# All sixteen sequences' gates of the delta rule in one batch, one write of the running decay sums, sum and cap as two operations in place

## The reference

```python
beta = jax.nn.sigmoid(bb)                          # bb, aa: [b, t, 8] projections of the normalised x
g = -jnp.exp(A_log) * jax.nn.softplus(aa + dt_bias)
alpha = jnp.exp(g)
def step(S, inp):
    q_t, k_t, v_t, beta_t, alpha_t = inp
    S = S * alpha_t[..., None, None]
    kv = jnp.einsum('bhk,bhkv->bhv', k_t, S)
    S = S + jnp.einsum('bhk,bhv->bhkv', k_t, (v_t - kv) * beta_t[..., None])
    return (S, jnp.einsum('bhk,bhkv->bhv', q_t, S))
```

## Time and profile before

| | us |
|---|---|
| three runs | 1888.81, 1888.66, 1886.35; median 1888.66 |
| the profiled execution's own time | 1888.68 |
| its span in the trace | 1887.0 (1.7 lie around it) |
| busy in the span | PE 1806.5, weight loads 1302.7, DVE 1174.6, ACT 709.8, POOL 669.4 |

### The profile page before, as it was taken

One profiled execution on the slowest core, in us unless ns is written; L12 is line 12 of the kernel. 1 busy time (PEld: TensorE's weight loads), 2 busy tenths in 40 slices (PEclk: granted clock), 3 DMA queues, 4 the chain that ended last, 5 costly groups with the idle time before them and its releaser, 6 DMA issues.

```text
span 1887.0 us, 39461 instructions
## 1 busy us (share of the span) xinstructions
PE 1806.5 (96%) x14800; PEld 1302.7 (69%) x14800; DVE 1174.6 (62%) x3215; ACT 709.8 (38%) x1887; POOL 669.4 (35%) x758
## 2 busy tenths in 40 slices
PE   6679999999889999999999999999999999999999
PEld 3357777776666666665445666666659979889698
DVE  5588888887656677677766667666665234243332
ACT  4124444444345555553001455655632222122221
POOL 3344443443216666674000376676624000000000
PEclk9879999999999999999999999999999999999999
DMA  6312212121022001010000000010040000000000
GB/s 195 53 33 49 39 34 43 37 42 26 13 79 71 25 27 36 26 35 11 1 1 1 10 29 20 20 29 20 11 179 1 3 7 1 10 1 1 10 1 10
DMA packets 98717, 58.61 MB, mean 31 GB/s; under 512 B 77801, under 2 KB 90465, under 8 KB 97761
## 3 DMA queue, kind: packets, MB, share of 16 engines
q1 hardware_dynamic: 98368, 56.03, 11.1%
q10 hardware_dynamic: 160, 0.06, 0.0%
HBM read 50.55 MB, written 5.51 MB: 30 GB/s over the span
## 4 chain that ended last, share of the span: by engine, by line
PE 81%; issue 5%; POOL 5%; DVE 4%; ACT 3%; DMA 1%; SPq 1%; DVEq 0%; POOLq 0%; ACTq 0%
PE ps L2582 18%; PE ps L1566 6%; PE ps L608 6%; PE ps L2454 5%; PE ps L1588 5%; PE ps L2114 5%; PE ps L1604 4%; PE ps L1643 4%; PE ps L1622 4%; PE ps L2660 3%; PE ps L728 2%; POOL w L580 2%; PE ps L1709 2%; PE ps L1575 2%; PE ps L1654 1%
## 5 line engine op out<-in xcount | busy, mean ns | idle before, releaser
L2027 POOL TENSOR_TENSOR h_w<-h_w 125x336 int32<-125x336 int32 x384 | 335.9, 904 | 210.4 <-ACT h_w L1808 210.4
L1912 DVE CUSTOM_DVE_ANT_0 h_w<-ps,h_w 112x375 f32<-112x375 f32 x512 | 263.3, 544 | 0.6 <-issue 0.3
L956 DVE SCALAR_TENSOR_TENSOR big_b<-ps,taps,big_b 128x444 f32<-128x444 f32 (+2 forms) x288 | 194.0, 674 | 74.9 <-ACT big_b L830 47.9
L1808 ACT ACTIVATE h_w<-ps 125x336 f32<-125x336 f32 x512 | 197.7, 468 | 21.7 <-PE ps L1588 21.7
L275 POOL TENSOR_TENSOR rstd<-var_eps,minus_half 112x4 f32<-112x4 f32 x12 | 12.2, 1015 | 406.5 <-DVE var_eps L262 406.5
L1588 PEld LDWEIGHTS ps<-h_w 32*125 32x125 f32 x3072 | 96.0, 183 | 62.1 <-issue 61.3
L1588 PE MATMUL ps<-h_w 32*125 32x112 f32 x3072 | 118.0, 282 | 7.8 <-DVE h_w L1912 5.5
L1921 DVE TENSOR_TENSOR h_w<-h_w,ps 128x112 f32<-128x112 f32 x128 | 34.7, 271 | 141.6 <-PE ps L1575 141.6
L1566 PE MATMUL ps<-h_w 32*112 32x375 f32 x1024 | 121.1, 519 | 0.8 <-DVE h_w L1912 0.8
L608 PE MATMUL ps<-h_w,w 128*128 128x448 f32 x256 | 110.3, 554 | 4.6 <-ACT h_w L852 4.6
L608 PE MATMUL ps<-h_w,kq_w 128*128 128x448 f32 x256 | 113.7, 569 | 0.0
(11 more groups left out here) (360 smaller groups left out, 3728.9 us busy)
## 6 DMA issues: line engine op xcount, KB each, us to landing
h_w<-in_h SPq DMA_DIRECT2D x2, 4096.0 KB, 17.0
kq_w<-in_ctxT SPq DMA_DIRECT2D x16, 375.0 KB, 3.4
h_w<-in_ctxT SPq DMA_DIRECT2D x16, 375.0 KB, 3.3
big_a<-decays SPq DMA_DIRECT2D x16, 196.0 KB, 3.2
w<-decays SPq DMA_DIRECT2D x16, 196.0 KB, 3.1
h_w<-in_mask SPq DMA_DIRECT2D x16, 164.1 KB, 3.3
kq_w<-in_kq_w SPq DMA_DIRECT2D x8, 256.0 KB, 3.7
w<-in_vz_w SPq DMA_DIRECT2D x8, 256.0 KB, 3.6
```

What stands on the lines that cost most here:

```text
L956: dve.scalar_tensor_tensor(p3(dst)[:, :, i:], p3(ps[:, bank, 0:GT])[:, :, 0:T - i], k.taps[:, h, n, TAPS - 1 - i:TAPS - i], p3(dst)[:, :, ...
L1808: act.activation(k.PTx[(4 * Q + r) % RING], ps[0:CK, turned_bank(Q, r), 0:NC * T], ACT.Exp).then_inc(s["exp"], 1)
L1912: dve.tensor_tensor_reduce(k.masked[r % 2], ps[0:T, score_bank(Q, r), 0:S2], k.mask_add[n % 2], -1.0, 3.0e38, ALU.add, ALU.min, k.neg_max[ ...
L2027: pool.tensor_tensor(P.bitcast(I32), P.bitcast(I32), k.mask_I[n % 2], ALU.mult).then_inc(s["weights"], 1)
```

## The change

The two batches become one of 16 sequences, so soft-plus, g, sums, bias and the write to DRAM are done once, with twice the columns (the sums fill 128 partitions). Every engine's opening order changes with it. `logs` becomes two POOL operations over 112x448 in place, an addition of the broadcast bias and a cap at 0, each signalled; ACT takes the exponential from that tile, and the tile is loaded again only after it (SP waits for gamma, not logs). POOL's opening order becomes logs(a+1), gammas(a).

```diff
-def start_dve_gate_in(dve, k, s, b):
+def start_dve_gate_in(dve, k, s):
...
+    dve.wait_ge(s["c_ba"], 48)
+    for g in range(NG):
+        dve.wait_ge(s["ba_t"], g + 1)
...
-def start_pe_cum(pe, k, s, b):
+def start_pe_cum(pe, k, s):
...
+    pe.matmul(k.ps[0:ALL, 5, 0:T], g, k.upto[:, :], start=True, stop=True).then_inc(s["cum_ps"], 1)
+    pe.matmul(k.ps[0:T, 6, 0:ALL], k.upto[:, :], g, start=True, stop=True).then_inc(s["cum_ps"], 1)
...
@@ gdn_pe
     start_pe_turn(pe, k, s, 1)
+    start_pe_tokens(pe, k, s, 0)
+    start_pe_gates(pe, k, s, 1)
+    start_pe_turn(pe, k, s, 2)
+    start_pe_tokens(pe, k, s, 1)
+    start_pe_gates(pe, k, s, 2)
     keys(0, 0)
-    start_pe_turn(pe, k, s, 2)
-    start_pe_gates(pe, k, s, 1)
+    start_pe_turn(pe, k, s, 3)
+    start_pe_tokens(pe, k, s, 2)
+    start_pe_gates(pe, k, s, 3)
     keys(0, 2)
-    start_pe_tokens(pe, k, s, 0)
-    start_pe_tokens(pe, k, s, 1)
-    start_pe_turn(pe, k, s, 3)
+    start_pe_tokens(pe, k, s, 3)
     keys(1, 0)
     keys(0, 4)
     pe.wait_ge(s["c_gdn"], 96)
-    start_pe_cum(pe, k, s, 0)
-    start_pe_gates(pe, k, s, 2)
+    start_pe_cum(pe, k, s)
     keys(1, 2)
-    start_pe_gates(pe, k, s, 3)
-    start_pe_tokens(pe, k, s, 2)
-    start_pe_tokens(pe, k, s, 3)
     keys(0, 10)
     keys(1, 4)
     keys(2, 0)
     keys(1, 10)
     keys(2, 2)
-    start_pe_cum(pe, k, s, 1)
@@ gdn_act
         elif slot == 3:
-            act.wait_ge(s["logs"], a + 1)
+            act.wait_ge(s["logs"], 2 * a + 2)
             if a:
                 act.wait_ge(s["gam"], a)
-            act.activation(k.gamma, k.soft[0:T, :, :].rearrange("p g t -> p (g t)"), ACT.Exp).then_inc(s["gamma"], 1)
+            act.activation(p3(k.gamma), k.cum[a % 2], ACT.Exp).then_inc(s["gamma"], 1)
...
     start_act_copy(act, k, s, 1)
+    start_act_gates(act, k, s, 1)
+    start_act_copy(act, k, s, 2)
+    start_act_gates(act, k, s, 2)
+    start_act_copy(act, k, s, 3)
+    start_act_gates(act, k, s, 3)
     act.wait_ge(s["c_gdn"], 96)
     keys(0, 0)
-    start_act_copy(act, k, s, 2)
-    start_act_gates(act, k, s, 1)
+    start_act_soft_plus(act, k, s)
     keys(0, 2)
-    start_act_soft_plus(act, k, s, 0)
-    keys(1, 0)
-    start_act_cum(act, k, s, 0)
-    start_act_copy(act, k, s, 3)
+    start_act_cum(act, k, s)
     act.wait_ge(s["setup_pool"], 1)
     exp_table()
-    start_act_gates(act, k, s, 2)
+    keys(1, 0)
     keys(1, 2)
     keys(0, 3)
-    start_act_gates(act, k, s, 3)
     keys(1, 3)
-    start_act_soft_plus(act, k, s, 1)
     keys(2, 0)
-    exp_table()
     keys(2, 2)
-    start_act_cum(act, k, s, 1)
     keys(2, 3)
@@ gdn_dve
     keys(0, 2)
-    start_dve_gate_in(dve, k, s, 0)
+    start_dve_gate_in(dve, k, s)
     keys(0, 3)
-    start_dve_gate_out(dve, k, s, 0)
+    start_dve_gate_out(dve, k, s)
     for a in range(1, AHEAD + 1):
         for slot in (2, 4, 3, 10):
             if a == 1 and slot == 2:
-                start_dve_bias(dve, k, s, 0)
+                start_dve_bias(dve, k, s)
             elif a == 1 and slot == 4:
                 keys(1, 3)
-            elif a == 3 and slot == 2:
-                start_dve_bias(dve, k, s, 1)
-            if a == 1 and slot == 10:
-                start_dve_gate_in(dve, k, s, 1)
-            elif a == 2 and slot == 2:
-                start_dve_gate_out(dve, k, s, 1)
@@ gdn_pool
-        if a:
-            pool.wait_ge(s["gamma"], a)
-        for j in range(G):
-            ins = pool.tensor_scalar(k.soft[0:T, j, :], k.cum[a % 2][:, j, :], k.gate_rows[:, 0, b, h, first + j:first + j + 1], 0.0,
-                                     ALU.add, ALU.min)
-        ins.then_inc(s["logs"], 1)
+        cum = k.cum[a % 2]
+        pool.tensor_tensor(cum, cum, k.gate_rows[:, 0, h, G * g:G * g + G].unsqueeze(2).to_broadcast([T, G, T]), ALU.add).then_inc(s["logs"], 1)
+        pool.wait_ge(s["logs"], 2 * a + 1)
+        pool.tensor_scalar(cum, cum, 0.0, None, ALU.min).then_inc(s["logs"], 1)
...
     for a in range(AHEAD):
+        logs(a + 1)
         gammas(a)
-        logs(a + 1)
         if a == NG + 1:
             join(pool, k, s, 0, 0)
@@ gdn_sp
-        if unit in (0, 2):
-            sp.wait_ge(s["cum_w"], 16 * (g // 2 + 1))
+        if unit == 0:
+            sp.wait_ge(s["cum_w"], 16)
         if unit >= 2:
-            sp.wait_ge(s["logs"], unit - 1)
+            sp.wait_ge(s["gamma"], unit - 1)
```

More of the change, by code:

```diff
@@ L44 @@
 UNITS = HEADS * NG
-BATCH = 2 * G
+ALL = B * HEADS
 LN_GDN, LN_MOE, LN_ATTN, LN_FFN = 0, 4, 8, 12
@@ L52 @@
 ba ba_sb ba_t ba_in soft_plus gates
-zeros proj_kq tap_kq conv_kq proj_vz tap_v conv_v cum_ps cum_sb cum_w cum_in0 cum_in1 logs kk tanh sz gamma gam kq N0 QG vtok W0
+zeros proj_kq tap_kq conv_kq proj_vz tap_v conv_v cum_ps cum_w cum_in0 cum_in1 logs kk tanh sz gamma gam kq N0 QG vtok W0
 nd_w0 nd_w1 ni_in c_in tri td_w pair_in pair off_w dn_in0 dn_in1 M_ps M R_ps R Y1 A Y2 less Y3 R_sum O squares o_var o_rstd On oT gated out gdn_x
@@ L303, in start_tiles @@
     flat = k.silu[0:T, :, :].rearrange("p a b -> p (a b)")
-    n = 2 * BATCH * HEADS
-    gates = [flat[:, i * n:(i + 1) * n].rearrange("p (b s h) -> p b s h", b=2, s=BATCH) for i in range(4)]
+    n = ALL
+    gates = [flat[:, i * n:(i + 1) * n].rearrange("p (s h) -> p s h", h=HEADS) for i in range(4)]
     mean_var = flat[:, 4 * n:4 * n + 2 * B].rearrange("p (s c) -> p s c", c=2)
@@ L318, in turn_banks @@
 def turn_banks(g):
-    return (5, 0) if g == 1 else (3, 4)
+    return (5, 0) if g % 2 else (3, 4)
 def gate_bank(g):
@@ L379, in start_dve_bias @@
+def start_dve_bias(dve, k, s):
     (y, t1, t2, bb), _, _, _, _ = start_tiles(k)
-    dve.wait_ge(s["cum_ps"], 2 * b + 1)
-    dve.scalar_tensor_tensor(k.gate_rows[:, 0, b], bb[:, b].rearrange("p s h -> p h s"), -1.0,
-                             k.ps[0:T, 6, 0:BATCH * HEADS].rearrange("p (h s) -> p h s", h=HEADS), ALU.mult, ALU.subtract).then_inc(s["gates"], 1)
-def start_pe_cum(pe, k, s, b):
[L387 to L394, removed]
@@ L397, in start_act_cum @@
[L397 to L402, removed]
+    dve.wait_ge(s["cum_ps"], 2)
+    dve.wait_ge(s["soft_plus"], 5)
+    dve.scalar_tensor_tensor(k.gate_rows[:, 0], bb.rearrange("p s h -> p h s"), -1.0,
+                             k.ps[0:T, 6, 0:ALL].rearrange("p (h s) -> p h s", h=HEADS), ALU.mult, ALU.subtract).then_inc(s["gates"], 1)
@@ new lines, in start_pe_cum, with start_act_cum @@
+def start_pe_cum(pe, k, s):
+    pe.wait_ge(s["gates"], 2)
+    g = k.gate_rows[:, 1].rearrange("p h s -> p (h s)")
+    pe.matmul(k.ps[0:ALL, 5, 0:T], g, k.upto[:, :], start=True, stop=True).then_inc(s["cum_ps"], 1)
+    pe.matmul(k.ps[0:T, 6, 0:ALL], k.upto[:, :], g, start=True, stop=True).then_inc(s["cum_ps"], 1)
+def start_act_cum(act, k, s):
+    act.wait_ge(s["cum_ps"], 1)
+    act.activation(k.cum_rows, k.ps[0:ALL, 5, 0:T], ACT.Copy).then_inc(s["setup_act"], 1)
+    act.wait_ge(s["setup_act"], 2)
+    act.dma_start(k.cum_d.rearrange("h s t -> (h s) t"), k.cum_rows).then_inc(s["cum_w"], 16)
@@ L427, in start_pe_gates @@
         pe.wait_ge(s["c_ba"], 48)
-    turned = g + 1 if g < 2 else NG
-    pe.wait_ge(s["lnT_act"], turned)
-    pe.wait_ge(s["lnT_dve"], turned)
+    pe.wait_ge(s["lnT_act"], g + 1)
+    pe.wait_ge(s["lnT_dve"], g + 1)
     for c in range(KD):
@@ L455, in start_act_gates, with start_act_soft_plus @@
     act.activation(k.gate_cols[g % 2], k.ps[0:16, gate_bank(g), 0:GT], ACT.Copy).then_inc(s["ba_sb"], 1)
-def start_act_soft_plus(act, k, s, b):
+def start_act_soft_plus(act, k, s):
     (y, t1, t2, bb), _, _, _, _ = start_tiles(k)
[L460 to L468, removed]
+    act.wait_ge(s["ba_in"], 1)
+    act.activation(t1, y, ACT.Abs).then_inc(s["soft_plus"], 1)
+    act.wait_ge(s["soft_plus"], 1)
+    act.activation(t1, t1, ACT.Exp, scale=-1.0).then_inc(s["soft_plus"], 1)
+    act.activation(bb, bb, ACT.Exp, scale=-1.0).then_inc(s["soft_plus"], 1)
+    act.wait_ge(s["soft_plus"], 2)
+    act.activation(t1, t1, ACT.Ln, bias=1.0).then_inc(s["soft_plus"], 1)
+    act.wait_ge(s["soft_plus"], 3)
+    act.activation(bb, bb, ACT.Ln, bias=1.0).then_inc(s["soft_plus"], 1)
 PER_SEQ = [slice(j * T, (j + 1) * T) for j in range(G)]
```

44 lines of the change are left out of this document (18 added, 26 removed).

## The result

| | before | changed |
|---|---|---|
| median of the runs, us | 1885.62 (8 runs, 1884.50 to 1888.81) | 1892.15 (8 runs, 1890.32 to 1893.89) |
| profiled execution, us | 1888.68 | 1890.46 |
| its span, us | 1887.0 | 1889.2 |

The ratio is 1.0030, 95% interval 1.0022 to 1.0039: the changed kernel is slower by some 5.7 us (the two medians are 6.5 apart). The forecast, 1893.0, lies 0.85 above the median, and its range holds it. But the profiled execution of before, on which the sum was built, stood 3 us above the median that more runs gave. As a difference, the forecast of +4.3 is 1.4 short of the ratio's 5.7 and 2.2 short of the medians' 6.5.

A forecast was written before the change was run, and what follows sets the result against it. The prediction took a chain over engines and queues to bound the opening (about 115 us) and PE the loop. Opening +5.6 and six joins -1.3 made +4.3 on 1888.68: 1893.0 us, range 1886.7 to 1900.0.

The forecast's parts named there:

- The opening: Stretch before the main loop, about 115 us, held by a chain over engines and queues: solve R 5.6 us later.
- six joins: In the loop, once per head, logs is a link of POOL's chain: 0.21 us saved each, -1.3 in all.
- The two operations: POOL's new logs: addition 1.14, wait 0.1, cap 1.14, together 2.36 us (1.85 to 3.05) against 2.57.
- The dear cap: Rival on POOL's logs: cap 1.8 us, logs 3.05, total +11.0, 1899.7 us; chance 0.20.
- the cheap cap: Rival on POOL's logs: cap at the memset's rate, logs 1.85, total +0.7, 1889.4 us; chance 0.20.
- First gates: First gate batch in the opening: all four groups turned first, so logs(0) starts at 45.2 us, 10.0 late.
- the dear step: In the first gates, ACT copies queries(0) after soft-plus, so DVE's 2.09 us query convolution stands ahead of g.
- Units 0 to 3: Opening's first units: N0(0) 11.4 us late, mostly given back, N0(3) at 69.7 against 66.05, +3.7.
- The rival of the delay given back: Rival on the opening: N0(3) comes 3 us sooner, total +0.6, 1889.3 us; chance 0.12.
- The two reordered triangles: POOL's opening: gammas(5) behind logs(6) makes gamma(6) 4.6 us late; gammas(7) behind logs(8) makes solve R 5.6 late.
- the prediction's two places: The places in the opening behind the reordered gammas, at gamma(6) and solve R, worth 1.9 us together.

The follow-up runs named there:

- e8: The changed kernel once more, without an edit: ratio 1.0028 to the kernel before.
- e3: The changed kernel with ACT's copy of queries(0) put back ahead of soft-plus: ratio 1.0006 to the kernel before.
- e6: The changed kernel with PE repeating unit 1's products of keys with keys six times more, to keep it at work: ratio 1.0010 to the kernel before.
- e1: The changed kernel with two triangles put back, gammas(5) before logs(6) and gammas(7) before logs(8): ratio 1.0008 to the kernel before.
- e2: The changed kernel with POOL's old order, gammas(a) before logs(a+1), for every a of the opening: ratio 1.0002 to the kernel before.
- e9: The changed kernel with both old orders, POOL's triangles ahead of logs and ACT's queries copy ahead of soft-plus: ratio 0.9989 to the kernel before.
- e4: The kernel before, with its two gate batches and POOL order, but the new two-operation logs and SP's wait on gamma: ratio 0.9984 to the kernel before.
- e7: e4 without the triangle product, the cap replaced by adding a mask of -1e30 above the diagonal: ratio 0.9963 to the kernel before.
- e10: e4 with SP loading the sums of unit 6 before exchange(0) instead of after it: ratio 0.9945 to the kernel before.
- e11: e7 with SP loading the sums of unit 6 before exchange(0): ratio 0.9920 to the kernel before.
- e5: The changed kernel with the cap done twice in every logs, each time waited for: ratio 1.0136 to the kernel before.

## Why the prediction was right, step by step

**Right in sum and in the places.** The opening was to be 5.6 late at solve R and was 5.0 (4.4 in e8's profile); six joins were to give 1.3 back and PE's waits shrank by 1.4. Both readings stand on the profiles; the total that they make, +3.7 at the last turn, agrees with the +4.3 forecast. (The prediction read R before as 113.4; the earlier trace rows has 113.49, so its own 119.0 is 5.5 late.)

**The two operations.** 2.36 predicted, 2.36 measured, but by errors that cancel: the cap was under-priced by 0.2 (1.335 for 1.14), the addition over-priced by 0.2 (0.93 for 1.14). The cap as one operation is neither at the memset's rate nor at that of the two-operation instructions; both rivals built on it fell. The dear cap wanted 1.8 and logs of 3.05; the cheap cap wanted the cap under 0.75. By the Trainium skill (GPSIMD Engine Reference, section Engine selection) GpSimd is about twice as slow as VectorE with two inputs, and one input goes roughly at line rate. For one input this does not hold in this trace: the one-input cap took 1.335 us, longer than the two-input addition over the same 448 columns, 0.93, and over twice VectorE's 0.62 for N0 of the same size.

**First gates.** Last tokens 30.7 predicted, 29.61 measured; g 38.9, 37.64; the load 41.6, 41.56; logs(0) 45.2, 44.68; N0(0) 51.1, 50.55. The early tokens are chance, for e3's came at 31.91. That the load agrees to 0.04 is luck as well: g came 1.3 sooner, but the write was issued 1.60 after it (37.64 to 39.24) where the prediction allowed 0.9 and the earlier trace rows had 1.40, and the load came 2.32 behind that instead of 1.8. e3 confirms the dear step, the query convolution ahead of g: 2.7 us.

**Units 0 to 3.** N0(3) at 69.7 predicted, 69.04 measured. That most of the 11 us are given back, because the second batch with its write is no longer in the way, held; so did the 3.2-us projection at the 1.2 GHz level, which e6 removed. The rival of the delay given back asked for 3 us more, which nothing gave.

**The two reordered triangles.** gamma(6) at 98.35 predicted, 97.68 measured; solve R 119.0, 118.53, and it is QG(7) behind gammas(7) that releases it, as said. e1 took them out and gained about 4 us by the timed runs, where the prediction's two places were worth 1.9 (0.9 at gamma(6) and 1.0 at solve R, each less the 0.2 that a shorter logs gives back). The profiles say less than the runs: from N0(3) to R it took 49.5 and 49.4 us in the two of the changed kernel and 46.8, 47.0 and 47.1 in e1, e2 and e9, so the order is worth 2.3 to 2.7 there; what is left to the timed 4 is within e1's interval (0.0009 either way). A link that the prediction did not name is part of it: N0(5) too stood behind gammas(5), started at 97.69 instead of 86.97 (e1), and PE's next projection then took 3.33 us after 9.80 of waiting, 1.68 in e1.

**What is left open.** By the traces the loss is 3.7 us at the last turn in the one profile and 3.0 in e8's; by the timed runs it is 5.7 and 5.3. Much of the gap is the profiled execution of before, which ran 3 us above its median: its logs(0) started at 35.19, where it started at 33.97, 33.60, 33.61 and 32.99 in the profiles of e4, e7, e10 and e11, whose gates are the same. Against these the changed kernel's logs(0), at 44.68, is 10.7 to 11.7 late and not 9.5. The sum was built on that one late execution, so that it came so near the median of the changed kernel is partly luck. Behind the last turn the profiles also differ: from 1370 to 1400 us the granted clock was 0.94 before, 1.00 in the changed kernel's profile, 0.94 in e8's, which is 1.8 us of one execution and none of the change.

## What to carry to other kernels

Merging instructions into one batch also moves what stands beside them in each in-order queue; here the loss came from two such moves (the triangle behind the logs, one copy behind soft-plus), and undoing both brought the batch to 0.9989, where the same logs with two batches stand at 0.9984: the merging itself saved nothing that can be told. In a chain over several engines, look in the queue of a DMA issuer for a transfer whose data and tile are ready and which stands behind one that waits: moving one load ahead gave more than the whole change cost. Before pricing an engine's link by its own length, check what the pause does to PE.

## What the hardware showed that was not expected

- In e5 six waits of PE of 1.29 us in the loop were each followed by a fall of the granted clock, 0.66 from 175 to 180 us behind the first, and cost more by it than by their own length (10.3 us on top of 7.1 for six). No such fall followed waits of 0.25 and 0.5 us: before and the changed kernel show 1.00 there. Length alone does not decide. A wait of 1.24 us at the loop's end (460 to 469 us, 492 in e5) had 1.00 behind it in before, the changed kernel, e8, e4 and e5. The same wait of 1.5 us before the next to last turn, 553.52 in the changed kernel and 551.89 in e1, was followed by a fall in the one profile and not in the other; here are the 10 us around it, first the changed kernel, then e1:

```profile
550.00:560.00 10.00, 8.09 (x50) 5.98 (x49) 4.71 (x11) 2.72 (x14) 1.82 (x3) 0.83 0.00 1
```

```profile
550.00:560.00 10.00, 7.24 (x48) 4.97 (x46) 5.22 (x12) 2.85 (x14) 2.12 (x4) 1.00 0.13 35
```

- On POOL a one-operation TENSOR_SCALAR of 112x448 took 1335 ns, a TENSOR_TENSOR addition of the same width 933, and one with the triangle 1136. In e7 the same addition of the mask took 1137 ns on the tile in big_a and 977 on the one in w:

```profile
L1147 POOL TENSOR_TENSOR big_a<-big_a,minus_upto 112x448 f32<-112x448 f32 x16 | 18.2, 1137 | 1.3
L1147 POOL TENSOR_TENSOR w<-w,minus_upto 112x448 f32<-112x448 f32 x16 | 15.6, 977 | 1.3
```

  Why the tile matters was not tried.
- POOL and DVE slowed each other where POOL's instruction ran beside a DVE TENSOR_TENSOR that reads and writes SBUF tiles. The cap took 1.84 us instead of 1.33 beside DVE's L554 (above), 0.53 us of which it shared with it; in e11 an addition took 2.09 instead of 0.93 beside a DVE product of 128x1372. The other way round, that DVE product (L580, L575) took 2.41 us in before and 2.23, 2.15 and 2.16 in e1, e2 and e9, where POOL's triangle had started just ahead of it, and 1.59 in the changed kernel, e8 and e3, where POOL was idle. No run moves one of the two alone, so this is read from where they overlap and not shown by an edit.
- How fast PE runs near 18 us differs between executions: the second group of gate rows took 3.14 us in e1, e3 and e9 and 1.66 in the six other profiles with one batch. In those three the last tokens were turned at 31.60 to 31.91, in the others at 29.25 to 30.48, so single profiles of an opening differ by up to 2.7 us before any edit acts.
